# The first tap of a depthwise convolution moved from VectorE to GpSimd

## What is computed

```python
# layer 0
xs = jnp.roll(_layer_norm(x, ln1_g, ln1_b), shift=(-3, -3), axis=(1, 2))
wins = ...                                    # windows of 49 tokens
q, k, v = ...                                 # wins @ qkv_w + qkv_b, 3 heads of 32
attn = jnp.einsum('whnd,whmd->whnm', q, k) + bias[None]     # and the mask of the shift
attn = jax.nn.softmax(attn, axis=-1)
out = jnp.einsum('whnm,whmd->whnd', attn, v)  # @ proj_w + proj_b, rolled back
x = shortcut + out
y = jax.nn.gelu(_layer_norm(x, ln2_g, ln2_b) @ fc1_w + fc1_b)
x = x + y @ fc2_w + fc2_b
# layer 1
y = jax.nn.relu(x)
y = lax.conv_general_dilated(y, dw_kernel, window_strides=(1, 1), padding='SAME',
                             feature_group_count=C)          # nine taps, one weight per channel each
y = y + dw_bias
y = ...                                       # pointwise C -> C, bias, batch norm
```

## Time and profile before

| | |
|---|---|
| median of 3 runs | 5510.72 us (5488.98 to 5522.0) |
| the profiled execution | 5488.53 us, span 5486.8 us |
| mean granted clock of TensorE | 0.993 of full speed |
| busy: TensorE, VectorE, ScalarE, GpSimd | 5291.6, 5129.3, 5060.9, 3786.2 us |
| instructions: TensorE, VectorE, ScalarE, GpSimd | 81186, 13773, 11038, 4105 |
| moved by DMA | 193.70 MB, mean 35 GB/s |

### The profile page before, as it was taken

One profiled execution on the slowest core, in us unless ns is written; L12 is line 12 of the kernel. 1 busy time (PEld: TensorE's weight loads), 2 busy tenths in 40 slices (PEclk: granted clock), 3 DMA queues, 4 the chain that ended last, 5 costly groups with the idle time before them and its releaser, 6 DMA issues.

```text
span 5486.8 us, 203158 instructions
## 1 busy us (share of the span) xinstructions
PE 5291.6 (96%) x81186; PEld 3789.4 (69%) x81186; DVE 5129.3 (93%) x13773; ACT 5060.9 (92%) x11038; POOL 3786.2 (69%) x4105
## 2 busy tenths in 40 slices
PE   5999999999999999999999999999999999999998
PEld 3767767676766676767777676767676767677675
DVE  4999999999999999999999999999999999999998
ACT  4999999999999999999999999999999989999996
POOL 3777767777777677777777677777777767777673
PEclk9999999999999999999999999999999999999998
DMA  1111111111111111111111111111111111111110
GB/s 25 34 36 35 36 36 37 35 36 35 36 35 36 35 36 35 36 35 36 36 35 38 36 36 35 36 35 36 36 36 36 37 34 36 36 35 36 37 36 24
DMA packets 275650, 193.70 MB, mean 35 GB/s; under 512 B 229160, under 2 KB 246041, under 8 KB 274713
## 3 DMA queue, kind: packets, MB, share of 16 engines
q1 hardware_dynamic: 274712, 180.70, 12.6%
HBM read 77.81 MB, written 77.07 MB: 28 GB/s over the span
## 4 chain that ended last, share of the span: by engine, by line
PE 57%; DVE 19%; ACT 12%; issue 6%; POOL 4%; SPq 1%; DVEq 0%; DMA 0%; ACTq 0%; POOLq 0%
PE bank L428 19%; PE bank L446 18%; DVE smax L819 7%; DVE prob L810 7%; PE bank L535 6%; PE bank L346 6%; PE bank L474 4%; ACT probT L635 4%; POOL prob L954 3%; ACT xT L663 3%; ACT o_tile L599 3%; PE bank L442 3%; DVE acc L850 2%; ACT prob L573 1%; POOL prob L963 1%
## 5 line engine op out<-in xcount | busy, mean ns | idle before, releaser
L850 DVE SCALAR_TENSOR_TENSOR acc<-ymap,taps,acc 96x784 f32<-96x784 f32 (+2 forms) x2176 | 2137.3, 987 | 54.9
L969 POOL TENSOR_TENSOR rstd<-var_eps,minus_half 112x7 f32<-112x7 f32 x512 | 1114.0, 2176 | 1266.0 <-DVE var_eps L883 1266.0
L428 PE MATMUL bank<-x1T,w 96*128 96x448 f32 (+1 forms) x3072 | 1148.3, 510 | 19.7 <-issue 10.5
L446 PE MATMUL bank<-hT,w 128*96 128x448 f32 (+1 forms) x3072 | 1097.1, 493 | 0.0
L627 ACT ACTIVATE hT<-bank,bfc 128x448 f32<-128x448 f32 (+1 forms) x1536 | 772.6, 564 | 11.9 <-PE bank L428 11.4
L428 PEld LDWEIGHTS bank<-x1T,w 96*128 96x128 f32 x3072 | 542.8, 190 | 346.6 <-issue 204.3
L954 POOL TENSOR_TENSOR prob<-prob,smax 128x392 f32<-128x392 f32 x768 | 653.6, 851 | 159.2 <-DVE smax L819 147.0
L980 POOL TENSOR_SCALAR xn<-x_in,minus_mean,rstd 112x96 f32<-112x96 f32 x768 | 680.9, 897 | 45.2 <-POOL offset L972 45.1
L446 PEld LDWEIGHTS bank<-hT,w 128*96 128x96 f32 x3072 | 466.3, 163 | 342.4 <-issue 165.4
L963 POOL TENSOR_TENSOR prob<-prob,srec 128x392 f32<-128x392 f32 x768 | 632.2, 852 | 81.7 <-DVE srec L828 81.7
L682 ACT ACTIVATE ymap<-bank,cols 96x128 f32<-96x128 f32 (+6 forms) x1056 | 603.2, 679 | 92.4 <-PE bank L446 92.4
(11 more groups left out here) (100 smaller groups left out, 10286.4 us busy)
## 6 DMA issues: line engine op xcount, KB each, us to landing
out<-o_tile SPq DMA_DIRECT2D x256, 210.0 KB, 2.5
x_in<-in_x SPq DMA_DIRECT2D x256, 168.0 KB, 2.9
x_in<-in_x SPq DMA_DIRECT2D x256, 126.0 KB, 2.9
k<-qk SPq DMA_DIRECT2D x512, 49.0 KB, 1.9
out<-o_tile SPq DMA_DIRECT2D x256, 84.0 KB, 2.5
hT<-in_L_conv_rel_bias SPq DMA_DIRECT2D x49, 0.6 KB
x1T<-in_L_conv_fc_w SPq DMA_DIRECT2D x1, 144.0 KB, 2.6
w<-in_L_conv_fc_w SPq DMA_DIRECT2D x1, 144.0 KB, 2.4
```

Of the source, the lines that this page charges most:

```text
L428: pe.matmul(bank[(1, 2, 5)[m]][:, 0:n * PT_], w1[:, m * 128:(m + 1) * 128], x1T[:, first * PT_:(first + n) * PT_], start=True, stop=True). ...
L446: mm = pe.matmul(bank[b][0:C, 0:n * PT_], w2[:, m, :], hT[:, m, first * PT_:(first + n) * PT_], start=False, stop=(m == MC - 1))
L850: last = dve.scalar_tensor_tensor(out=dst, in0=src, scalar=taps[:, i:i + 1], in1=dst, op0=ALU.mult, op1=ALU.add)
L969: pool.tensor_tensor(b["rstd"][:], b["var_eps"][:], minus_half[0:PT_], ALU.pow)\
```

## The change

Tap 0 leaves VectorE's queue. GpSimd gets a function `first_tap` with the same product as a tensor_scalar of its own, called at the head of its step. A new semaphore `tap_begun` counts it once per strip, and VectorE's tap 1 waits for that; `tap_done` now counts eight taps per strip, and the waits on it in `pointwise` and `into_map` are renumbered. The two waits of tap 0, for the map and for the accumulator's last reader, move with it.

```diff
--- before.py
+++ after.py
@@ -187,7 +187,7 @@
         parts_done = [sem("parts1_done"), sem("parts2_done")]
         halves_done = [sem("halves1_done"), sem("halves2_done")]
         ln_ready = [sem("ln1_ready"), sem("ln2_ready")]
-        tap_done = sem("tap_done")
+        tap_done, tap_begun = sem("tap_done"), sem("tap_begun")
 
         shifted, p_ready = sem("shifted"), sem("p_ready")
         rstd_done = [sem("rstd1_done"), sem("rstd2_done")]
@@ -514,7 +514,7 @@
                     return
                 first, n = HALVES[i]
                 if i == 0:
-                    wait(pe, tap_done, nth(t - 4, 9, 8))
+                    wait(pe, tap_done, nth(t - 4, 8, 7))
                 wait(pe, q_ready, nth(t + 1, 2, i))
                 if not has(t + 1):
                     wait(pe, ymap_ready, nth(t - 2, 2, i))
@@ -668,7 +668,7 @@
                 s = t - 1
                 first, n = ((0, 4), (4, 3))[half]
                 if half == 0:
-                    wait(act, tap_done, nth(t - 4, 9, 8))
+                    wait(act, tap_done, nth(t - 4, 8, 7))
                 area = area_of_strip(s)
                 if s % NWIN == NWIN - 1:
                     parts = [(0, 4, area + 2), (4, 3, area + 7)]
@@ -835,20 +835,16 @@
                 dy, dx = i // 3 - 1, i % 3
                 top = area_below_strip(c) + 1 + dy
                 low = top + TOP_ROWS + ((c + 1) % NWIN + 1) // NWIN
-                if i == 0:
-                    wait(dve, ymap_ready, nth(c + 1, 2, 1))
-                    wait(dve, pw_psum, nth(t - 5, 2, 1))
+                if i == 1:
+                    wait(dve, tap_begun, nth(c, 1, 0))
                 else:
-                    wait(dve, tap_done, nth(c, 9, i - 1))
+                    wait(dve, tap_done, nth(c, 8, i - 2))
                 parts = ((top, 0, TOP_ROWS), (low, TOP_ROWS, LOW_ROWS)) if low > top + TOP_ROWS else ((top, 0, WS),)
                 for row, at, n in parts:
                     src = ymap[:, row:row + n, dx:dx + HW]
                     dst = acc[0:C, (phase + 1) % 2, at:at + n, :]
-                    if i == 0:
-                        last = dve.tensor_scalar(dst, src, taps[:, 0:1], None, ALU.mult)
-                    else:
-                        last = dve.scalar_tensor_tensor(out=dst, in0=src, scalar=taps[:, i:i + 1], in1=dst,
-                                                        op0=ALU.mult, op1=ALU.add)
+                    last = dve.scalar_tensor_tensor(out=dst, in0=src, scalar=taps[:, i:i + 1], in1=dst,
+                                                    op0=ALU.mult, op1=ALU.add)
                 last.then_inc(tap_done, 1)
 
             def values(t, phase, i):
@@ -919,7 +915,6 @@
                 add_up(t, 1)
                 add_up(t, 2)
                 values(t, phase, 1)
-                tap(t, phase, 0)
                 norm_x(t, phase)
                 tap(t, phase, 1)
                 tap(t, phase, 2)
@@ -962,6 +957,20 @@
                 r = srec[:, at].unsqueeze(2).broadcast_to([128, PAIRS, NT])
                 pool.tensor_tensor(p, p, r, ALU.mult).then_inc(p_ready, 1)
 
+            def first_tap(t, phase):
+                c = t - 3
+                if not has(c):
+                    return
+                top = area_below_strip(c)
+                low = top + TOP_ROWS + ((c + 1) % NWIN + 1) // NWIN
+                wait(pool, ymap_ready, nth(c + 1, 2, 1))
+                wait(pool, pw_psum, nth(c - 2, 2, 1))
+                parts = ((top, 0, TOP_ROWS), (low, TOP_ROWS, LOW_ROWS)) if low > top + TOP_ROWS else ((top, 0, WS),)
+                for row, at, n in parts:
+                    last = pool.tensor_scalar(acc[0:C, (phase + 1) % 2, at:at + n, :],
+                                              ymap[:, row:row + n, 0:HW], taps[:, 0:1], None, ALU.mult)
+                last.then_inc(tap_begun, 1)
+
             def root(which, s):
 
                 b = ln[which]
@@ -1000,6 +1009,7 @@
                     rest(1, t, x1n, x1[:, t % 2], x1n_rest)
 
             def step(t, phase):
+                first_tap(t, phase)
                 divide(t, 0)
                 divide(t, 1)
                 divide(t, 2)
```

## The result

| | before | after |
|---|---|---|
| median | 5508.85 us (4 runs, 5488.98 to 5522.0) | 6335.86 us (4 runs, 6294.61 to 6371.23) |
| ratio of times, 95% interval | | 1.150 (1.142 to 1.158) |
| profiled execution, span | 5486.8 us | 6345.5 us |
| mean granted clock of TensorE | 0.993 | 0.917 |

The change makes the kernel 15% slower, 827 us. The forecast had the direction and about a sixth of the size: 5640 us, and its range ended at 5785.

What follows compares the result with a forecast made beforehand. A per-strip chain through TensorE, VectorE, GpSimd and ScalarE, GpSimd's third division without slack, bounds the kernel. 5488.5 + 142 (253 x 0.56) - 1 = 5629.5, plus half of a 22 us offset: 5640 us, range 5550 to 5785.

Steps and rivals of the forecast that it cites:

- the price of TensorE's waits through its clock: TensorE was to wait about 0.5 us more a strip; no term or case covered its granted clock.
- The ring: Chain repeating every 20.86 us strip: TensorE's scores, VectorE's additions and maxima, GpSimd's shift, ScalarE, TensorE's weighing and MLP; no tap.
- the edge: End of GpSimd's third division lies on the repeating chain without slack worth counting; its 2.27 us of idle time lie behind.
- a strip grows by D - 0.44 us, 253 times: Divisions late by D - 0.42, less some 0.02 in the weighing: 0.56 us a strip, 142 us in 253 strips.
- The duration D: Length of GpSimd's new 96x784 tensor_scalar, put at 1.0 us from the memset's slope, 0.844 ns an element.
- the last of its bounds: If all over 203 ns in the 96-element tensor_scalar row were elements: 2.5 ns an element, 2.1 us for GpSimd's tap.
- the heavier rival: GpSimd's tap lasts 2.1 us, delay 1.68 us a strip: 5908 us, or 6030 with port interference; chance 0.10.
- VectorE's relief: Removing tap 0 frees 0.94 us of VectorE's queue a strip, worth nothing at the end where attention runs.
- So GpSimd pays beside VectorE instructions with two SBUF inputs, and VectorE doesn't: GpSimd's tensor_scalar slows (1121 against 425 ns median) beside taps L850, which stay at 1083 ns at most.
- The extra 0.5 us of the heavier rival: Third division, from about 2516.3, would meet VectorE's first two-input tap at 2516.6 and pay up to 0.5 us: 6030 us.
- the prediction's own signs of being wrong: VectorE's wait for L346 not growing, the division's delay vanishing before L474, or the new GpSimd instruction over 1.5 us.
- the formula's cases from D = 0.76 to 1.51: GpSimd's tap as pure memset, 0.76 us (5569 us), up to the two-input slope, 1.51 us (5760 us).

Runs made afterwards that it cites:

- experiment 2: The kernel after with first_tap called behind the three divisions instead of ahead of them; 5504.1 us against 5503.8 for the kernel before, ratio 1.000.
- experiment 3: The kernel before, VectorE's nine taps kept, plus an unread 96x784 tensor_scalar on GpSimd between third shift and first division; 6397.3 us against 5503.8.
- four lengths: The kernel before plus an unread GpSimd tensor_scalar of 98, 288, 448 or 560 elements ahead of the divisions; 5519.8, 5635.2, 5722.0 and 5800.5 us.
- the instruction of 1.005 us: The kernel before plus an unread GpSimd tensor_scalar of 288 elements between third shift and first division; 5635.2 us, ratio 1.025.
- experiment 4: The filled kernel: the kernel after with TensorE doing its transposes of x1n three times; 5929.3 us against 5503.8 for the kernel before, ratio 1.078.
- experiment 9: The kernel before plus an unread GpSimd tensor_scalar of 672 elements between third shift and first division; 5959.5 us, ratio 1.084.
- experiment 1: The kernel before with tap 0 left out on VectorE and nothing added on GpSimd; 5483.8 us against 5503.8, ratio 0.996.
- experiment 10: Against the kernel before, tap 0 split: five rows on GpSimd behind the divisions, two on VectorE at the old place; 5503.1 us against 5501.7.
- experiment 11: Against the kernel before, tap 0 split: four rows on GpSimd behind the divisions, three on VectorE; 5506.7 us against 5506.0, ratio 1.001.

## Why the prediction was wrong

Two terms of the sum failed: the duration of GpSimd's instruction, 1.0 us where 2.24 were measured, and the price of TensorE's waits through its clock, which stood at nothing and came to 407 us.

**The ring and the edge: right.** No tap in the ring, the third division with no slack, the tap between shift and division by the order of the calls; GpSimd's idle time behind it. Experiments 2 and 3 show it both ways, and the formula "a strip grows by D - 0.44 us, 253 times" holds within 24 us for four lengths. With D = 1.0 the forecast had a loss of 142 us, and the instruction of 1.005 us lost 134.

**The duration D: the first term that failed.** "With one tensor in and one out I take the memset's slope on the tensor_scalar's base ... D = 1.0 us." It measured 2.24. The slope is 2.5 ns an element, not 0.844. The prediction had this number, as the last of its bounds: (425 - 203) / 89 = 2.5 ns an element and 2.1 us, from the only row of the operation itself. It stood as the heavier rival at 0.10 and 5908 us; the filled kernel, which has its delay without the clock, came to 5929. I chose the memset's and tensor_tensor's rows because their slopes fit a tidy picture of one access per cycle. The nearest row was the one of the same operation. The Trainium skill (GPSIMD Engine Reference, Engine selection) calls operations with one input roughly line-rate; by these runs this one takes about three times the memset's time per element.

**The clock: the second term, missing altogether.** The prediction let TensorE wait in every strip and priced the wait alone. It is half of the loss, 407 of 827 us. Nothing in the trace of before could show where the clock gives way, but that more waiting could cost it was not among the cases. The Trainium skill (TensorE: Matmul & The Clock Gate, A second HAM failure mode: psum-queue depth-cycling) describes short idle times between groups of matmuls that make the clock swing; experiments 3, 4 and 9 (672 elements, clock 0.978) agree with it, in a float32 kernel and with waits for another engine.

**VectorE's relief worth nothing: nearly.** 20 us of a possible 240 (experiment 1).

**"So GpSimd pays beside VectorE instructions with two SBUF inputs, and VectorE doesn't": wrong for the small sums.** In the kernel after, the divisions reach VectorE's sums of two SBUF inputs. VectorE's timeline, against the divisions that end at about 3019.6 and 3020.4:

```profile
3018.94 0.72 DVE L869 TENSOR_TENSOR sum<-stats 112x7 f32<-112x7 f32 x1
3019.58 0.88 DVE L870 TENSOR_TENSOR diff<-stats 112x7 f32<-112x7 f32 x1
3020.39 0.16 DVE L871 TENSOR_TENSOR dev<-stats 112x7 f32<-112x7 f32 x1
...
3021.01 5.34 DVE L846 SCALAR_TENSOR_TENSOR acc<-ymap,taps,acc 96x784 f32<-96x784 f32 x5
```

The first two each last until a division ends, where they took 0.17 us before. That is the exclusive lock of the Trainium skill (SBUF — State Buffer, Who interferes with whom), which the prediction had set aside for the row of L850. Here it lay in VectorE's slack: VectorE still waited 577 us for the scores. The extra 0.5 us of the heavier rival did not come, because the held sums put the first tap on VectorE at 3021.01, behind the end of the third division at 3020.44. One of the prediction's own signs of being wrong, an instruction over 1.5 us long, is what the trace shows.

**The range.** It held the formula's cases from D = 0.76 to 1.51 and left out a case that its own rows supported. Had it reached to that rival's 6030, it would still have missed by 306 us, as no case in it held a price for the clock.

## What to carry to other kernels

An idle engine's share says nothing about where its idle time lies: put moved work behind the instruction that others wait for, and read from the order of the calls, not from the name of the change, on which side it lands. Price an operation by the row of the same operation, however short, before reasoning from its neighbours. And where a change makes TensorE wait in every iteration, price the granted clock as a case of its own: here waits of 1.23 us in a strip of some 22.6 (0.45 before) went with 407 us lost through the clock, nearly as much as the 425 through the delay.

## What I had not expected of the hardware

- GpSimd's tensor_scalar in float32 with one scalar per partition takes about 0.30 us and 2.5 ns an element, more per element than its tensor_tensor with two inputs (1.68).
- TensorE's clock is at 0.989 with waits of 0.35 + 0.16 + 0.16 us a strip, at 0.978 with 0.63 + 0.16 + 0.16 and at 0.917 with 0.91 + 0.16 + 0.16, and repeated transposes in the gap bring it back to 0.995.
- A VectorE tensor_tensor with two SBUF inputs, 0.17 us long, is held until a GpSimd tensor_tensor ends (0.72 and 0.88 us), but only to 0.54 us beside a tensor_scalar of 2.25 us (experiment 2). The taps L850, with two SBUF inputs as well, were hardly ever held (1083 ns at most). What decides between them is open.
- VectorE's tensor_scalar is quicker and held beside GpSimd's division with two rows of 112, slower and not held with three (1.00 and 0.55 us). The Trainium skill (SBUF — State Buffer, Who interferes with whom) says that tensor_scalar contends where it runs in a mode that uses both ports; experiments 10 and 11 agree, and the switch lies between two rows and three here.
